# Attention over edges: the 0/1 matrices formed by ScalarE (squared distance, then the positive part of one less that) instead of by a comparison on VectorE

## The reference, cut to what matters

```python
q = (node_attr @ Wq).reshape(n, H, DQ // H)
x_src = node_attr[src]
k = _conv_per_edge(x_src, edge_attr, edge_sh, Wang_k, Wlin_k, W1k, b1k, W2k)   # per edge
v = _conv_per_edge(x_src, edge_attr, edge_sh, Wang_v, Wlin_v, W1v, b1v, W2v)   # per edge
alpha = jnp.einsum('ehq,qk,ehk->eh', q[dst], Wdot, k)
amax = jax.ops.segment_max(alpha, dst, num_segments=n)
ealpha = jnp.exp(alpha - amax[dst])
denom = jax.ops.segment_sum(ealpha, dst, num_segments=n)
out = jax.ops.segment_sum((ealpha / denom[dst])[..., None] * v, dst, num_segments=n)
```

## Time and profile before

| | |
|---|---|
| median of 3 runs | 5351.29 us (5340.92 to 5359.75) |
| the profiled execution's own time | 5396.27 us |
| its span | 5394.5 us |
| busy share of the span | PE 79%, PEld 65%, DVE 56%, ACT 36%, POOL 36% |
| mean granted TensorE clock | 0.881 |

### The profile page before, as it was taken

How to read it: one execution, slowest core, us unless ns; L and a number is a source line. 1 busy time by engine, 2 the same in 40 slices (tenths; PEclk the granted TensorE clock), 3 DMA queues, 4 the chain that set the end, 5 groups by cost and what they waited for, 6 DMA issues and landing times. The chain is left out here.

```text
span 5394.5 us, 73118 instructions
## 1 busy us (share of the span) xinstructions
PE 4256.8 (79%) x26543; PEld 3492.6 (65%) x26543; DVE 3031.5 (56%) x4164; ACT 1931.3 (36%) x2481; POOL 1918.9 (36%) x2002
## 2 busy tenths in 40 slices
PE   4658999999999846777778777777777787777842
PEld 4657999999999734565556556555655566566632
DVE  8985444444453424555555655555655656555644
ACT  5655655665565312222222222222222222222213
POOL 5630000000000065544444544445544555545343
PEclk9779999999999957888888988888988889988875
DMA  7989999999995334545454554545554555544433
GB/s 185 206 190 285 290 299 287 297 292 291 292 294 186 113 87 126 149 137 143 142 144 140 147 143 136 146 140 146 149 147 140 146 150 148 151 140 141 137 116 48
DMA packets 1014256, 950.03 MB, mean 176 GB/s; under 512 B 705661, under 2 KB 811913, under 8 KB 1013763
## 3 DMA queue, kind: packets, MB, share of 16 engines
q1 hardware_dynamic: 951955, 814.30, 51.5%
q0 software_dynamic: 61936, 130.95, 10.0%
HBM read 655.09 MB, written 289.56 MB: 175 GB/s over the span
## 5 line engine op out<-in xcount | busy, mean ns | idle before, releaser
L2263 POOL DMA_INDIRECT e_x_rows<-x_table,src_s x1616 | 1546.6, 957 | 1553.4 <-PE e_turn_ps L2375 1101.7
L1254 PE MATMUL acc<-t_wide,scaled 128*128 128x448 f32 x6860 | 1417.1, 367 | 24.4 <-DVE t_wide L1347 24.4
L1254 PEld LDWEIGHTS acc<-t_wide,scaled 128*128 128x128 f32 x6860 | 1284.4, 188 | 137.4 <-DVE scaled L1365 24.7
L1289 ACT CAST t_wide<-t_ring 128x1568 fp32r<-128x1568 uint8 x490 | 737.3, 1505 | 572.8 <-PE acc L1254 555.0
L1347 DVE CAST t_wide<-t_ring 128x1568 fp32r<-128x1568 uint8 x490 | 478.5, 977 | 748.5 <-PE acc L1254 731.8
L2303 PE MATMUL e_turn_ps<-e_weighted,e_spot 128*128 128x128 f32 x3232 | 516.2, 326 | 298.6 <-issue 287.4
L2303 PEld LDWEIGHTS e_turn_ps<-e_weighted,e_spot 128*128 128x128 f32 x3232 | 477.8, 235 | 337.6 <-issue 326.3
L2439 ACT COPY e_out_rows<-e_turn_ps 128x1024 f32<-128x1024 f32 x202 | 204.4, 1012 | 919.0 <-remote 576.5
L1721 POOL MEMSET l_wdot<- 64x64 f32 x1 | 0.1, 148 | 1459.8 <-POOLq L1453 1459.8
L2503 DVE TENSOR_TENSOR e_x_gk<-e_ring_ps,e_x_t 128x1024 f32<-128x1024 f32 x202 | 247.2, 1224 | 471.7 <-remote 387.0
L2354 PE MATMUL e_ring_ps<-e_wlin_v,e_x_gv 128*128 128x128 f32 x3232 | 459.8, 297 | 50.9 <-issue 46.4
(11 more groups left out here) (273 smaller groups left out, 5108.9 us busy)
## 6 DMA issues: line engine op xcount, KB each, us to landing
t_ring<-adjacency_bytes SPq DMA_DIRECT2D x490, 512.0 KB, 5.7
sums_table<-e_out_rows SPq DMA_DIRECT2D x202, 576.0 KB
q_first<-hop_zeros_q SPq DMA_DIRECT2D x101, 512.0 KB, 5.9
e_sh<-parts_sh SPq DMA_DIRECT2D x404, 128.0 KB
e_ea<-parts_ea SPq DMA_DIRECT2D x404, 128.0 KB
e_q_rows<-q_first SPq DMA_DIRECT2D x404, 128.0 KB
e_same<-same_row SPq DMA_DIRECT2D x404, 128.0 KB
adjacency_bytes<-lists_staged SPq DMA_DIRECT2D x196, 256.0 KB
```

What stands on the lines that cost most here:

```text
L1254: mm = nc.tensor.matmul(acc[c][:, 0:n], U[p][:, b, :], wide[m % WIDE_RING][:, lo:lo + n], start=(b == 0 and p == 0), stop=(b == NB - 1 and ...
L1289: nc.scalar.copy(into, of).then_inc(wide_act, 1)
L2263: nc.gpsimd.indirect_dma_start(x_rows[i % XR][:, g * GT + t, :], None, x1_table, bass.IndirectOffsetOnAxis(ap=src_ix[:, at:at + 1], axis=0 ...
```

## The change

A 0/1 entry is now max(0, 1 - (f - place)^2). As f and place are integers, the square is 0 or at least 1, so the result is exactly 1 or 0. ScalarE forms the squares in eight instructions, one for each tile of 128 edges, because the bias operand holds one value for each partition, and the positive part in one instruction over all eight tiles. The pieces:

- A new tile `apart` [128, 8, 128] holds the squares; a constant column `one` is set by VectorE once.
- ScalarE's queue: `measure_spots(i+1-LAG)` stands between `keep_weights` and `keep_hidden`; `find_spots(i+1-LAG)` stands right behind `keep_hidden`. Each is thus for the round that TensorE spreads out one iteration later.
- VectorE's `find_spots` (copy and comparison) is gone, and the spare columns of `e_score_ps` with it.
- TensorE: `scores` no longer waits for `v_spot`; `spread_out` waits for `a_spot` as well.

```diff
+        apart = sb("apart", [P, K, P])
-        score_ps = ctx.enter_context(nc.psum_tensor("e_score_ps", [P, 2 * P + K], F32))
+        score_ps = ctx.enter_context(nc.psum_tensor("e_score_ps", [P, 2 * P], F32))
...
             def spread_out(j, i):
                 pe.wait_ge(v_weighted, j + 1)
+                pe.wait_ge(a_spot, j + 1)
...
             def scores(i):
                 n, p = divmod(i, BATCH)
                 pe.wait_ge(v_prod, i + 1)
-                if on(i + 1 - LAG):
-                    pe.wait_ge(v_spot, 2 * (i + 1 - LAG) + 2)
...
+            def measure_spots(j):
+                if j >= 1:
+                    act.wait_ge(a_spot, j)
+                for k in range(K):
+                    last = nc.scalar.activation(apart[:, k, :], iota[:], ACT.Square, scale=-1.0,
+                                                bias=fpos[:, j * K + k:j * K + k + 1])
+                last.then_inc(a_apart, 1)
+
+            def find_spots(j):
+                act.wait_ge(a_apart, j + 1)
+                if j >= 2:
+                    act.wait_ge(p_seg, j - 1)
+                nc.scalar.activation(spot[j % 2][:], apart[:], ACT.Relu, scale=-1.0, bias=one[:, 0:1]).then_inc(a_spot, 1)
+
+            act.wait_ge(const, 12)
             for i in ITERATIONS:
...
                 if chain_at(i - 2) is not None:
                     keep_weights(chain_at(i - 2))
+                if on(i + 1 - LAG):
+                    measure_spots(i + 1 - LAG)
                 if on(i + 1):
                     keep_hidden(i + 1)
+                if on(i + 1 - LAG):
+                    find_spots(i + 1 - LAG)
...
-            def find_spots(i, j):
-                dve.wait_ge(p_score, min(i - 1, N))
-                nc.vector.tensor_copy(score_ps[:, 2 * P:2 * P + K], fpos[:, j * K:(j + 1) * K]).then_inc(v_spot, 1)
-                if j >= 2:
-                    dve.wait_ge(p_seg, j - 1)
-                dve.wait_ge(v_spot, 2 * j + 1)
-                nc.vector.tensor_tensor(spot[j % 2][:], iota[:].unsqueeze(1).to_broadcast([P, K, P]),
-                                        score_ps[:, 2 * P:2 * P + K].unsqueeze(2).to_broadcast([P, K, P]),
-                                        ALU.is_equal).then_inc(v_spot, 1)
...
                 if on(j):
-                    find_spots(i, j)
                     weigh(i, j)
```

More of the change, by code:

```diff
@@ L2078, in edge_attention @@
         iota = sb("iota", [P, P])
+        one = sb("one", [P, 1])
         x_rows = [sb(f"x_rows{s}", [P, K, D]) for s in range(XR)]
@@ L2132, in edge_attention @@
         v_gk, v_gv, v_q, v_rkq, v_prod = sem("v_gk"), sem("v_gv"), sem("v_q"), sem("v_rkq"), sem("v_prod")
-        v_spot, v_lw, v_weighted = sem("v_spot"), sem("v_lw"), sem("v_weighted")
+        v_lw, v_weighted = sem("v_lw"), sem("v_weighted")
+        a_apart, a_spot = sem("a_apart"), sem("a_spot")
         v_top, v_most, v_drop, v_lsum = sem("v_top"), sem("v_most"), sem("v_drop"), sem("v_lsum")
@@ L2495, in _ @@
             nc.vector.tensor_copy(iota[:], iota_i[:]).then_inc(const, 1)
-            dve.wait_ge(const, 11)
+            nc.vector.memset(one[:], 1.0).then_inc(const, 1)
+            dve.wait_ge(const, 12)
             def gate(i):
```

## The result

The changed kernel takes 5522.9 us (median, 5513.57 to 5534.89), the kernel before 5346.1 us on the same chip: ratio 1.032, interval 1.029 to 1.035, 177 us slower. The profiled execution has a span of 5513.2 us, 119 us more than the profiled execution of the kernel before, which was 45 us above its median.

A forecast was written before the change was run, and what follows sets the result against it. Bound: transposes, eight gathers, about 1.8 us until TensorE's result is seen, the copy, transposes again. VectorE -6, setting the constant +1, other terms 0: 5351 - 5 = 5346 us; range 5270 to 5390.

The forecast's parts named there:

- only after the round's gathers: Attention rounds: what TensorE has finished reaches other engines only after the eight gathers; short iteration 15.2 us, floor 14.3.
- the third rival: TensorE's results come free in gather steps of 1.26 us; a quarter of rounds shifting: 63 us, either sign; chance 0.20.
- the part on the path: Before line 2526: of VectorE's removed 300 us, up to 60 could count; a tenth, 6 us, was taken as gain.
- the rival that VectorE's 1.5 us count: Copy and comparison before line 2526 delay TensorE: 60 us gain, 150 if in all late-release rounds; chance 0.20.
- 2.3 fit in both: Between keep_x and the Relus: eight squares, 2.3 us, fit ScalarE's idle 3.24 us (short iteration) and 6.92 (long).
- I take 0 on the path: ScalarE's added 3.4 us a round, squares and positive part, cost no time; up to 2 us in all.
- My slower rival: At a_hid, before line 2303: Relus late if squares and other preceding work exceed 3.24 us; at most 145 us; chance 0.10.
- the 3.75 us of line 2303 in the long iteration: Line 2303 starts only behind both Relus, at 4052.41, and its 3.75 us add to the long iteration of 19.2 us.
- Three of those named for "right": Signs: idle before line 2526 up 1.5 us a round; ScalarE +690, VectorE -280 us; gathers' end 1.7 us before line 2439's copy.
- The sign for "wrong" that fired: Before line 2303: a sum of waits differing from 287 us by more than 20 would show the forecast wrong.
- The rule on which engine should do it: By the skill's rule, 1.5 us become 3.4; if ScalarE's queue set the end, up to 384 us slower.
- Put at no more than 0.05 us a round: TensorE: one wait goes before line 2333, one comes before line 2303; 0, within 10 us in all, either sign.

The follow-up runs named there:

- c2_no_spots: The kernel before, with the 0/1 matrices formed only in the first two rounds and nothing added to ScalarE, on a late chip: 5352 us, ratio 0.999.
- c_no_spots: The kernel before, with the 0/1 matrices formed only in the first two rounds and nothing added to ScalarE, on a prompt chip: 4366 us, ratio 1.000.
- h_wait_more: The kernel before with one more TensorE wait before line 2303, for the long-met v_lw, on a late chip: 5477 us, ratio 1.001.

## Why the prediction was wrong

**What bounds the rounds.** That TensorE's results become visible late, and that this, not an engine's work, closes the rounds on this chip, was in the rows and holds: GpSimd's gathers are unchanged and the loss sits in the waits around them. The rule drawn from it, that a result reaches the others "only after the round's gathers", came from two iterations and holds for the late copies of the sums (115 of 116). It does not hold for the Relus: of 106 late ones in the kernel before, 78 start in the midst of the gathers. They start mostly near a gather's end, which fits the steps of the third rival. That the gathers cause the lateness stays untested, as the two kernels made for it ran on prompt chips. There, copies and Relus follow at once while the gathers run, so gathers alone do not suffice. The lateness is the chip's as much as the kernel's: the same kernel takes some 1000 us less on another. A smaller slip: 1.32 us from gather to gather is an average over an iteration in which one gather took 1.40; otherwise the step is 1.26.

**VectorE.** The 300 us of work went, and the part on the path was put at 6 us; c2_no_spots measures 0.999 (0.997 to 1.001) and c_no_spots 1.000 (0.999 to 1.001). Right. So the rival that VectorE's 1.5 us count is out.

**ScalarE, the step that failed.** The prediction said that the squares fit between `keep_x` and the Relus: "2.3 fit in both", "I take 0 on the path". Prices and fit were right (393 and 1146 ns, and 5.58 us of idling behind the squares in the long round). The conclusion was not. The same work, read by nobody, costs 2.6% on a late chip. The squares do not hold ScalarE when the result is there (in the changed kernel one Relu of 202 starts straight behind them); with them ahead of the Relus, the result is there later. My slower rival had the right place, `a_hid`, and the wrong mechanism: it was to decide only once the squares, with what else precedes the Relus, exceeded 3.24 us, and eight of them take 2.44. Nearest is the third rival, "the releases fall otherwise": 39 more Relus start over 3 us late. I gave it 63 us, no sign, and little shifts in TensorE's waits as its cause. The runs show a sign, later; another cause, ScalarE's eight squares ahead of the Relus; and some 140 to 180 us (ratios 1.025 to 1.032). By what path ScalarE's work delays a result of TensorE stays open.

**The clock.** The prediction took the 3.75 us of line 2303 in the long iteration as a given, and no term for more such rounds was in the sum. There are 94 instead of 59, and the group is busy 57 us longer.

**The signs.** Three of those named for "right" came: VectorE's idle time before line 2526 grew from 367.5 to 682.2 us, 1.6 us a round, busy times moved as said, and the copy of the sums still follows the eighth gather, by 2.1 us at the median (2.0 before). They tell that the work moved, not that the move is free. Line 2468 came later behind the transposes, 7.5 us on average instead of 7.0. The sign for "wrong" that fired is the wait before the multiplication: 129 us more, against a limit of 20.

**The rule on which engine should do it.** The rule of the Trainium skill, "ScalarE: Activation LUTs", section "Rules for kernel authors", that relu and the like belong on VectorE, comes out on the right side here. The work took 1.4 us a round on VectorE and 3.6 on ScalarE. But it was not by the path I gave it: ScalarE's queue did not set the end. And the tables were no issue: no table load appears in the attention stage but the one there was before.

**TensorE's waits.** Put at no more than 0.05 us a round; the start moved by 0.15. On a prompt chip that would be 30 us, 0.7%, as read from the rows. On a late chip it cannot be told from nothing (h_wait_more, 1.001).

**The range.** 5270 to 5390, with 0.20 for slower. The rows showed a mechanism whose onset I could not explain, and the range treated it as noise of 63 us.

## What to carry to other kernels

Idle time of an engine is room for its own work, but it is not proof that work put there is free: where the trace shows results that reach the other engines microseconds behind their recorded end, test an added instruction by itself, ahead of that wait and behind it. Try one large instruction instead of eight small ones there, or put them behind the wait: here these kernels came to 1.006 and 1.002, where the eight ahead of the wait cost 1.026. Count a wait over all rounds before two of them are made a rule. Where TensorE sets the pace, look at which instruction the wait that is met last sits on. And take a ratio on more than one chip before it is called a property of the kernel.

## What the runs showed of the hardware that I had not expected

- One kernel took 4364 to 4366 us on three chips and 5346 to 5467 us on three others. The gathers took 957 to 962 ns on both kinds, and the mean granted clock of the kernel before was 0.94 to 0.95 against 0.87 to 0.90.
- On the late chips TensorE's results reached ScalarE up to 14 us behind their modelled end, on the prompt ones 0.04 us. Of 106 Relus that started over 1 us late in the kernel before, 78 started while the gathers ran, mostly near a gather's end.
- Behind 3.08 us without work TensorE's granted clock was 0.50, and sixteen instructions took 3.75 us instead of 1.95. Late results thus cost twice: 88 us more idling and 27 us more busy time.
- Eight ScalarE instructions of 393 ns ahead of a wait for such a result (with one of about 1.15 us behind it) cost 2.6% on a late chip and 0.2% on a prompt one; one of 1156 ns in their place left 0.6% on the late chip, in a kernel that also had the fourth wait.
- With a fourth wait ahead of line 2303, the wait that is met last stood alone ahead of another instruction of waits, and the weight load began 0.22 us behind the end of the second Relu instead of 0.07; with that wait written first it began 0.05 us behind it.
